# The clip of two exponentials moves from GpSimd to VectorE, with a new order of units on every engine

## What is computed

```python
W = -w * t_rem
e = jnp.exp(jnp.clip(W + K, -20.0, 10.0))
past_attention = jnp.cumsum(e * V, axis=1)
past_energy = jnp.cumsum(e, axis=1)
eu = jnp.exp(jnp.clip(U.reshape(1, 1, H, HS) + K, -20.0, 10.0))
A = shift(past_attention) + eu * V
B = shift(past_energy) + eu
WKV = A / B
out = (jax.nn.sigmoid(R) * WKV).reshape(n, t, -1) @ Wo.T + bo
```

```python
x = x + _L0_attn_a_ref(_layernorm(x, axis=-1), ...)
x = x + _L0_ffn_ref(_layernorm(x, axis=-1), ...)
x = x + _L0_attn_b_ref(_layernorm(x, axis=-1), ...)
x = x + _L0_ffn_ref(_layernorm(x, axis=-1), ...)
```

## Time and profile before

| what | us |
|---|---|
| median of 3 runs | 2376.15 |
| lowest and highest | 2371.28, 2376.19 |
| the profiled execution, its own time | 2375.18 |
| its span in the trace | 2373.4 |

### The profile page before, as it was taken

How to read it: one execution, slowest core, us unless ns; L and a number is a source line. 1 busy time by engine, 2 the same in 40 slices (tenths; PEclk the granted TensorE clock), 3 DMA queues, 4 the chain that set the end, 5 groups by cost and what they waited for, 6 DMA issues and landing times. The chain is left out here.

```text
span 2373.4 us, 21200 instructions
## 1 busy us (share of the span) xinstructions
PE 1597.9 (67%) x4800; PEld 768.9 (32%) x4800; DVE 1864.1 (79%) x2430; ACT 920.8 (39%) x1470; POOL 1249.9 (53%) x939
## 2 busy tenths in 40 slices
PE   4352496578855797586955798566965777586757
PEld 1110242333422342243413353233423343243424
DVE  3187897897879898887979988888978968985462
ACT  2343345243633346233543336333452425232321
POOL 0547538752596437843496426854387434741150
PEclk9575698788977898787967899777977888887878
DMA  4322422113311413113311313204221122110100
GB/s 141 145 86 89 134 75 80 54 60 111 104 63 34 151 41 109 49 35 136 101 58 44 122 58 105 71 27 140 79 75 53 51 98 82 45 36 25 38 9 9
DMA packets 124953, 179.33 MB, mean 76 GB/s; under 512 B 10481, under 2 KB 74482, under 8 KB 124850
## 3 DMA queue, kind: packets, MB, share of 16 engines
q1 hardware_dynamic: 124850, 178.36, 22.6%
HBM read 140.05 MB, written 38.27 MB: 75 GB/s over the span
## 5 line engine op out<-in xcount | busy, mean ns | idle before, releaser
L534 POOL TENSOR_TENSOR bu<-rep,bc 128x512 f32<-128x512 f32 x512 | 673.4, 1344 | 571.7 <-PE ps_y L968 535.2
L778 DVE TENSOR_TENSOR_SCAN ps_d<-ps_d,bu 128x512 f32<-128x512 f32 x512 | 625.2, 1221 | 79.9 <-ACT ps_d L645 54.6
L645 ACT ACTIVATE ps_d<-rep,scale_a 128x512 f32<-128x512 f32 x512 | 348.5, 688 | 530.9 <-DVE bu L785 517.4
L907 PE MATMUL ps_r<-mix,wkv 128*128 128x512 f32 x512 | 274.2, 684 | 160.4 <-DVE kv L850 158.1
L968 PE MATMUL ps_y<-bu,sel 128*32 128x512 f32 x1024 | 177.9, 775 | 281.2 <-DVE bu L785 281.1
L785 DVE TENSOR_TENSOR bu<-ps_d,bc 128x512 f32<-128x512 f32 x512 | 344.7, 675 | 0.0
L907 PEld LDWEIGHTS ps_r<-mix,wkv 128*128 128x128 f32 x512 | 107.0, 220 | 322.1 <-issue 320.3
L907 PE MATMUL ps_r<-xT,wgate 128*128 128x512 f32 x384 | 198.7, 642 | 11.8 <-ACT xT L648 11.8
L546 POOL TENSOR_TENSOR kv<-sums,kv 128x1024 f32<-128x1024 f32 x64 | 150.2, 2347 | 106.1 <-DVE sums L864 106.1
L907 PE MATMUL ps_r<-xT,wup 128*128 128x512 f32 x384 | 183.9, 601 | 0.0
L916 PE MATMUL ps_r<-wo,yr 128*128 128x256 f32 x512 | 159.4, 475 | 31.1 <-DVE yr L876 31.1
(11 more groups left out here) (93 smaller groups left out, 2280.0 us busy)
## 6 DMA issues: line engine op xcount, KB each, us to landing
rep<-dd_scratch SPq DMA_DIRECT2D x128, 512.0 KB, 4.3
dd_scratch<-xs SPq DMA_DIRECT2D x32, 512.0 KB, 3.1
bc<-bc_scratch SPq DMA_DIRECT2D x64, 256.0 KB, 4.9
xc_scratch<-xc SPq DMA_DIRECT2D x32, 256.0 KB, 2.0
sz_scratch<-xin SPq DMA_DIRECT2D x32, 256.0 KB, 2.1
xg<-xc_scratch SPq DMA_DIRECT2D x32, 256.0 KB, 2.7
szg<-sz_scratch SPq DMA_DIRECT2D x32, 256.0 KB, 2.9
wr<-w_r_dram SPq DMA_DIRECT2D x64, 128.0 KB, 3.2
```

The lines of the kernel that those rows point to most:

```text
L534: pool.tensor_tensor(bu[:, i % BU, :], rep[:, g % REP, 1, :], bc[:, 0, q, :], ALU.mult)\
L645: act.activation(ps_d[D_BANK[i]][:, :], rep[:, g % REP, 0, :], ACT.Exp, scale=scale_a[:, a, NQ * j + q:NQ * j + q + 1]).then_inc(decay_rea ...
L778: dve.tensor_tensor_scan(d[:, :], d[:, :], bu[:, i % BU, :], 0.0, ALU.mult, ALU.add)\
L907: last = pe.matmul(dst, lhs, rhs, start=n == 0, stop=n == len(pairs) - 1)
```

## The change

The unit `g_clip` leaves GpSimd's list and its code. A unit `v_clip` with the same waits, the same operands and the same bounds stands in VectorE's list. All five lists of `ORDER` are replaced, with the same units otherwise. `R_USES`, the tiles and all other instructions stay.

```diff
-          "v_kd.1 v_ev.0 v_esum.0 v_evsum.0 v_hc.19 v_kd.2 v_scan.21 v_hc.20 v_scan.22 v_ev.1 v_wkv.0 "
+          "v_scan.16 v_hc.15 v_scan.17 v_sz.2 v_hc.16 v_gate.0 v_scan.18 v_kd.0 v_hc.17 v_scan.19 v_clip.0 "
+          "v_kd.1 v_ev.0 v_esum.0 v_evsum.0 v_sz.3 v_hc.18 v_scan.20 v_clip.1 v_hc.19 v_ev.1 v_wkv.0 "
...
-                    elif unit == "g_clip":
-
-                        pool.wait_ge(eu_ready.sem, at(eu_ready, r, i + 1))
-                        pool.wait_ge(e_ready.sem, at(e_ready, r, i + 1))
-                        pool.sem_inc(carried.sem, 1)
-                        pool.tensor_scalar(rows(i, "e", "eu"), rows(i, "e", "eu"), float(np.exp(np.float32(HI))),
-                                           float(np.exp(np.float32(LO))), ALU.min, ALU.max).then_inc(clipped.sem, 1)
...
+                    elif unit == "v_clip":
+                        dve.wait_ge(eu_ready.sem, at(eu_ready, r, i + 1))
+                        dve.wait_ge(e_ready.sem, at(e_ready, r, i + 1))
+                        dve.sem_inc(carried.sem, 1)
+                        dve.tensor_scalar(rows(i, "e", "eu"), rows(i, "e", "eu"), float(np.exp(np.float32(HI))),
+                                          float(np.exp(np.float32(LO))), ALU.min, ALU.max).then_inc(clipped.sem, 1)
```

## The result

The changed kernel takes 2387.28 us (median of four runs, 2387.00 to 2390.29), the kernel before 2373.72 in the same comparison (2369.30 to 2376.19): a ratio of 1.0062, with an interval of 1.0042 to 1.0082. It is slower by 0.6%, 13.6 us. The profiled executions differ by 11.8 us (spans 2385.2 and 2373.4).

What follows compares the result with a forecast made beforehand. VectorE was taken to bound the pass, helped by TensorE before attention and GpSimd in it. Terms summed to +3.3 us a pass, 19.8 in six, and -3 in the last program: 2392 us, own range 2381 to 2408, overall 2350 to 2420.

Steps and rivals of the forecast that it cites:

- The clips, +4.8: VectorE in attention: eight clips at 0.6 us of its time each add 4.8 us a pass.
- what they meet, +2.4: Six of eight clips meet queued GpSimd work, 0.4 us each: +2.4 us a pass, bounds 0 and 18.7.
- Relief of the running sums, -1.0: GpSimd, 9.2 us less in the way, disturbs VectorE's running sums less: -1.0 us a pass, bounds -3 and 0.
- Waits that go, -12.0: VectorE's attention waits for GpSimd's clip, add and product (3.2, 4.0, 2.8) and for a decay (2.0) vanish each pass.
- come, +5.3, +1.3, +1.5: New VectorE waits a pass: output projection's first addition 5.3 us, tile 4's quotient 1.3, tile 5's key projection 1.5.
- The start of a pass, +1.0: Reordered stretch before attention, output projection's second half first on VectorE: +1.0 us a pass, between -4 and +6, least certain.
- The sum of a pass, +3.3: All terms together lengthen each loop pass by 3.3 us, 19.8 us in six passes.
- Behind the loop: Two programs after the loop: the first gains and loses like a pass; the last, without scans, saves 3 us.
- The faster case: TensorE at full clock at the output projection, no late reciprocal or key projection: -2.6 us a pass, 2357 us; chance 0.30.
- The heavy case: Each clip stands behind GpSimd's running instruction and runs at the two-input rate: 2410 to 2445 us; chance 0.11.
- the second rival: New waits just eat the old, a pass within 0.7 us of unchanged: 2372 to 2380 us; chance 0.13.
- The signs named: Expected in the new profile: clip times, GpSimd waits under 3 us, addition and quotient waits, a pass of 276 us.

Runs made afterwards that it cites:

- the order alone: The changed kernel with its new order kept but the clips put back on GpSimd: 2423.47 us, ratio 1.0216.
- the move alone: The kernel before, its order kept, with each clip moved to VectorE directly in front of its first reader: 2362.00 us, ratio 0.9962.
- the statistics first: The changed kernel with the new sequence's statistics put first on VectorE in a pass: 2406.36 us, ratio 1.0145.
- the cover: The changed kernel with v_hc.25, v_scan.27 and v_hc.26 moved between tile 3's quotient and the output projection's first addition: 2404.43 us, ratio 1.0136.
- one clip twice: The changed kernel with the clip of tile 1 done twice in a row on VectorE: 2416.98 us, one execution.

## Why the prediction was right, and where its steps were not

The time came out 4.7 us under the 2392 forecast, on the forecast side. That the total came so near is luck. The prediction put 19.8 us into the passes and -3 behind them; the traces show 1.6 in the six passes and filling, and 10.2 behind. Two errors of opposite sign cancelled: the passes grew by almost nothing in place of 3.3 us each, and the draining programs by 10.2 in place of -3. The mechanisms in attention held, their sizes in part. Step by step:

- **The clips, +4.8, and what they meet, +2.4.** The base was right: 660 to 694 ns undisturbed. What they meet was under-sized. In the pass above they take 9.33 us, which with 0.08 of overlap each is 8.7, so +3.9 beside +4.8. Half of that excess is one clip behind an add, with the add's own row on GpSimd:

```profile
1215.86 2.69 DVE L841 TENSOR_SCALAR kv<-kv 128x1024 f32<-128x1024 f32 x1
```

```profile
1215.65 2.35 POOL L539 TENSOR_TENSOR kv<-sums,kv 128x1024 f32<-128x1024 f32 x1
```

  The add ends at 1218.00, the clip 0.55 us later, a little less than a clip takes: it stood until the add was done. By the Trainium skill ("SBUF — State Buffer", section "Who interferes with whom") the shared ports go to one engine for its whole instruction; this row agrees. The prediction weighed that rule against 2.4 and priced it at 9.6. Measured is 3.9: two more clips (1.63 and 1.65 us) started when an add had some 1.1 us left and also end 0.55 us after it, and five were not held up.
- **Relief of the running sums, -1.0.** It is -3.2: sixteen of them take 26.5 us in a pass after, 29.7 before. They take 26.3 in the run with the order alone and 27.9 with the move alone, so the order brings more of it than GpSimd's lighter load. The term was outside its bounds by a little (-3 to 0) and its reason was half wrong.
- **Waits that go, -12.0, and come, +5.3, +1.3, +1.5.** All waits of VectorE for GpSimd in attention are gone, and 1.2 of the 2.0 for a decay. The addition waits 6.06 us (forecast 5.2 to 6.2), the quotient behind it 1.28 (1.3). All waits for key and value projections together are 0.7; the forecast had 1.5 more for tile 5 beside the 1.3 that was to stay. All waits in the stretch fell from 15.2 (13.3 in the earlier trace rows and 1.9 in three smaller rows of that view) to 8.9, -6.3, where the prediction's terms give -3.9.
- **The start of a pass, +1.0.** The first decay step comes 94.0 us into the pass, 94.6 before: -0.6. But two units of VectorE that stood ahead of it before, `v_hc.17` and `v_sz.3`, 0.6 us each, stand behind it now. Like for like the start is 0.6 longer, well inside the bounds. The prediction had the hidden part the wrong way round: the first half of TensorE's output is there after 5.6 us, not 4.5, and the turn hides behind it (see the run with the statistics first).
- **The sum of a pass, +3.3.** In attention the measured terms and the two units that moved into it give 8.7 - 3.2 - 6.3 + 1.2 = +0.4, and from the first decay step to the last addition of the output projection the pass is 0.4 longer. With -0.6 ahead of it and +0.2 behind it nothing is left over, and the pass is +0.02. Against the forecast the clips cost 1.5 more, and the sums (2.2), the waits (2.4) and the start (0.4, like for like) gave more than was put down.
- **Behind the loop.** Here the prediction failed. It let the first draining program gain and lose like a pass and then left its 3.3 out of the sum, a plain slip; and like a pass it is not. VectorE waits there 2.1 us in all for GpSimd's clips, products and adds before the change, in these three rows, against 10.0 in a pass, so there was little to win against the cost of the clips and the addition's wait:

```profile
DVE kv L850 <- POOL kv L541: 1.0, 1, 1.0
...
DVE yr L876 <- POOL kv L552: 0.7, 1, 0.7
...
DVE sums L858 <- POOL kv L546: 0.4, 1, 0.4
```

  For the last program it gave the clips -3 and took the order as neutral. The move alone changes nothing there (215.4 in both), and VectorE's new list costs 3.6. The third place of the order shown ahead of the prediction was read for the loop only.
- **The rivals.** The faster case rested on the move winning more than it costs; that is true of the move (269.7), not of the change. The heavy case's mechanism, a clip behind an add, happens to three clips in eight, and to one of them for nearly the whole add. That the change "balances" to an even pass was the second rival, within 0.7 us, and for the passes it is what happened.
- **The signs named.** Clip 0.7 alone: seen. 1.1 beside GpSimd: 1.6 and 2.7. Waits for GpSimd under 3: none. The two waits at the addition: seen. A pass of 276: 273.07. Of what would have made it wrong nothing occurred, so those three signs could not tell a pass of 276 from one of 273.

What stays open: why settled passes lie 3.41 us apart in most kernels, and why three kernels, two of the old order and one of the new, do not settle. All four lengths are whole multiples of that distance (79, 80, 81 and 83 times), and nothing here shows what keeps them there. The step from 273.07 to 276.48 was followed through its rows in three kernels (the order alone, the cover, one clip twice), where a second group at the lower clock is part of it; the steps to 269.65 and 283.3 show no such group. That the clock makes all steps is argued, not shown.

## What to carry to other kernels

Price a program behind a loop from its own waits, not from the loop's: a wait that a change removes in the steady state may not exist there, while what it adds is paid in full. When a change bundles a move with a new order, forecast the two apart, since here a gain and a loss of some 3.4 us made a pass that looked untouched, and the move alone was worth 0.4%. Where TensorE comes out of an idle stretch just ahead of the work that others wait for, a start one microsecond later cost three here, and a start one microsecond earlier cost as much. When a sum comes out right, check its parts: this one was right by two errors.

## What the runs showed of the hardware

- The settled passes of one kernel agree within 0.15 us, often within 0.03, and those of most kernels lie at 269.65, 273.07, 276.48 and 283.3 us; a single added clip on VectorE moved the pass by 3.41, taking eight away by the same 3.41. In other kernels the passes alternate (271.2 and 271.5) or wander (274.5 to 278.5, 266.3 to 268.4).
- TensorE, idle for 12 us in front of the output projection, made its first group at the lower of its two clocks, 1.2 GHz (3.78 us for eight products), and the next at 2.4 GHz (1.99). The next group stayed at 3.78 when the start was 1.1 us later in the pass, and also when it was 1.3 us earlier, after 9.2 us of idle time. The Trainium skill ("TensorE: Matmul & The Clock Gate", section "Part 1: The HAM clock gate (the "warmup" mystery)") says that the clock is gated by how busy the array has been recently; a first group at the lower clock behind 12 us of idle time agrees with that, and nothing here shows more of it.
- A one-input VectorE instruction over 1024 elements took 2.69 us when a GpSimd add of 2.35 us had begun 0.2 us earlier, 1.63 when it had begun 1.3 us earlier, and 0.66 alone; held up, it ended 0.55 us after the add each time. The other way round, an add that began 0.2 us after such a clip took 2.65 us.
- The turn of the loop keeps VectorE from its first instruction for 4.0 to 5.3 us, over all kernels, where that one waits for nothing else (4.33 in the earlier trace rows). An instruction that waits 5.6 us for TensorE anyway loses nothing by it: 5.57 us in a pass, 5.58 in the last program, where there is no turn.
